# Turning the rotated keys of a tile by a transposing DMA instead of TensorE

## What is computed

```python
q = jnp.einsum('bsd,ed->bse', x, Wq).reshape(bsz, seqlen, HQ, D)
k = jnp.einsum('bsd,ed->bse', x, Wk).reshape(bsz, seqlen, HK, D)
v = jnp.einsum('bsd,ed->bse', x, Wv).reshape(bsz, seqlen, HK, D)
q = _rope(_rmsnorm(q, q_norm_w), pos)
k = _rope(_rmsnorm(k, k_norm_w), pos)
k_all = jnp.concatenate([k_cache[block_table], k], axis=1)
v_all = jnp.concatenate([v_cache[block_table], v], axis=1)
scores = jnp.einsum('bqhd,bkhd->bhqk', q, k_all) * SCALE
scores = jnp.where(valid, scores, -1e+30)
probs = jax.nn.softmax(scores, axis=-1)
o = jnp.einsum('bhqk,bkhd->bqhd', probs, v_all)
return jnp.einsum('bse,de->bsd', o, Wo)
```

## Time and profile before

| | us |
|---|---|
| median of three runs | 2203.47 |
| lowest and highest | 2203.23, 2203.65 |
| the profiled execution | 2202.7 |
| its span, first to last instruction | 2200.7 |
| TensorE busy | 2151.3 |
| VectorE busy | 1694.2 |
| ScalarE busy | 1486.1 |
| GpSimd busy | 1222.4 |
| mean granted TensorE clock | 0.995 |

### The profile page before, as it was taken

How to read it: one execution, slowest core, us unless ns; L and a number is a source line. 1 busy time by engine, 2 the same in 40 slices (tenths; PEclk the granted TensorE clock), 3 DMA queues, 4 the chain that set the end, 5 groups by cost and what they waited for, 6 DMA issues and landing times.

```text
span 2200.7 us, 61088 instructions
## 1 busy us (share of the span) xinstructions
PE 2151.3 (98%) x17966; PEld 1409.9 (64%) x17966; DVE 1694.2 (77%) x3917; ACT 1486.1 (68%) x4982; POOL 1222.4 (56%) x2070
## 2 busy tenths in 40 slices
PE   6989899999999999999999999999999999999998
PEld 3545466666666666666666666666666666666665
DVE  8785587777777777777777777787777777777785
ACT  5844487776676776777666666666777666666664
POOL 6002156655655556665566565666665565666563
PEclk9999999999999999999999999999999999999999
DMA  8988576766767666666778676666666666666563
GB/s 233 290 281 262 180 209 199 208 189 211 210 194 210 195 201 204 192 207 191 210 235 252 187 239 190 178 187 176 181 178 175 180 188 175 177 187 178 175 183 102
DMA packets 478831, 440.12 MB, mean 200 GB/s; under 512 B 52885, under 2 KB 407524, under 8 KB 477734
## 3 DMA queue, kind: packets, MB, share of 16 engines
q1 hardware_dynamic: 433062, 295.67, 46.0%
q0 software_dynamic: 40960, 134.25, 19.9%
q10 hardware_dynamic: 4480, 6.29, 1.0%
HBM read 377.21 MB, written 56.70 MB: 197 GB/s over the span
## 4 chain that ended last, share of the span: by engine, by line
PE 86%; DVE 1%; issue 0%; ACT 0%; DVEq 0%; ACTq 0%
PE PR L1323 22%; PE Op L1304 15%; PE WOp L1362 15%; PE Sp L1270 15%; PE PTp L1281 11%; PE TRp L1336 3%; PE Sp L1273 2%; PE Op L1286 1%; PE Op L1306 1%; PE TRp L1347 1%; DVE masked L1514 0%; PE WOp L1347 0%; ACT masked L1419 0%; DVE WoT L1573 0%; DVE OT L1532 0%
## 5 line engine op out<-in xcount | busy, mean ns | idle before, releaser
L735 POOL DMA_INDIRECT pages<-values_split,rows x512 | 525.0, 1025 | 104.0 <-issue 77.7
L1413 ACT ACTIVATE pts<-PTp 128x512 f16<-128x512 f32 x512 | 305.7, 597 | 364.4 <-PE PTp L1281 363.6
L1323 PE MATMUL PR<-Wt,xT 128*128 128x512 f16 x2232 | 539.0, 380 | 0.0
L1304 PEld LDWEIGHTS Op<-pts,pages 128*128 128x128 f16 x6144 | 385.3, 98 | 121.6 <-DVE OT L1532 4.4
L1304 PE MATMUL Op<-pts,pages 128*128 128x128 f16 x6144 | 426.7, 219 | 2.6 <-DVE OT L1532 2.4
L1270 PE MATMUL Sp<-pages,qT 128*128 128x512 f16 x1536 | 415.8, 380 | 6.5 <-PEq L185 6.5
L1514 DVE CUSTOM_DVE_ANT_0 masked<-Sp,mask 128x544 f32<-128x544 f32 x512 | 370.2, 723 | 60.2 <-PE Sp L1273 54.3
L1519 DVE TENSOR_TENSOR pts<-PTp,pts 128x512 f16<-128x512 f32 x512 | 351.6, 687 | 74.7 <-ACT pts L1413 74.1
L1419 ACT ACTIVATE masked<-masked,small 128x544 f32<-128x544 f32 x512 | 379.0, 740 | 8.1 <-DVE small L1514 7.7
L1362 PE MATMUL WOp<-WoT,OT 128*128 128x512 f16 x1536 | 377.5, 379 | 0.0
L1532 DVE TENSOR_TENSOR OT<-Op,OT 128x128 f16<-128x128 f32 x512 | 148.3, 290 | 265.5 <-ACT p L1407 261.9
(11 more groups left out here) (252 smaller groups left out, 3019.2 us busy)
## 6 DMA issues: line engine op xcount, KB each, us to landing
pages<-keys_transposed SPq DMA_DIRECT2D x2048, 64.0 KB
mask<-mask_rows SPq DMA_DIRECT2D x128, 128.0 KB, 3.8
v<-new_values SPq DMA_DIRECT2D x96, 128.0 KB
weights_split<-wdst SPq DMA_DIRECT2D x40, 256.0 KB, 4.7
keys_transposed<-pages SPq DMA_DIRECT2D x32, 256.0 KB, 4.7
values_split<-pages SPq DMA_DIRECT2D x16, 512.0 KB, 3.6
rope_s<-rope_table SPq DMA_DIRECT2D x32, 256.0 KB, 3.3
pages<-values_split,rows POOLq DMA_INDIRECT x512
```

The source lines that it names most:

```text
L735: nc.gpsimd.indirect_dma_start(out=vS[:, n % 2, c, :, :].rearrange("p l n -> p (l n)"), out_offset=None, in_=v_d, in_offset=bass.IndirectO ...
L1304: nc.tensor.matmul(o, vS[:, par, c, low, h * D:(h + 1) * D], pts[:, u % 2, part, c * P:(c + 1) * P], start=(k == 0), stop=False)
L1323: m = nc.tensor.matmul(bank(k), xT[:, c, xl, :], Wp[:, c, wl, GROUP_COL[k]:GROUP_COL[k] + HID], start=(i == 0), stop=(i == NPASS - 1))
L1413: nc.scalar.activation(pts[:, u % 2, 0, :], PTp[:, :], ACT.Copy).then_inc(G.pt_hi, 1)
```

## The change

The rotated keys (group 0) no longer go through TensorE. In slot 6 ScalarE copies `qr` to f16 in its natural order into a new buffer `split` and VectorE puts the low part beside it. At the end of slot 14 ScalarE's queue issues one transposing DMA from `split`, 128 partitions x 1024 f16, into `kTn`: eight blocks of 128x128, four heads high and four heads low. The next tile's first scores wait for it, and so does the next tile's write to `split`. The query groups are turned as before; their semaphore counts leave the keys out. To make room for `split`, four small tables of the first block move into the buffer of the output weights, which is free then.

```diff
+QUERY_GROUPS = len(NORMED) - 1
...
-    turn={5: 0, 6: 1, 10: 3, 12: 4, 14: 5}, turned={6: 0, 7: 1, 11: 3, 13: 4, 15: 5},
+    keys=14, turn={6: 1, 10: 3, 12: 4, 14: 5}, turned={6: 0, 7: 1, 11: 3, 13: 4, 15: 5},
...
+        split = sb("split", [P, 2, HID], F16)
...
-        seqf = sb("seqf", [P, B], F32)
-        wq_b = sb("wq_b", [P, D], F32)
-        wk_b = sb("wk_b", [P, D], F32)
...
-        stacked = sb("stacked", [P, 3 * P // 2], F32)
...
-        jump = scr[:, 2880:2944]
+        seqf, wq_b, wk_b, stacked = scr[:, 2880:2944], scr[:, 7168:7296], scr[:, 8064:8192], scr[:, 3392:3584]
...
+            def turn_no(ti, k):
+                return ti * QUERY_GROUPS + NORMED.index(k) - 1
...
                         if u % UPT == 0 and u > 0:
-                            pe.wait_ge(G.tr_lo, len(NORMED) * (u // UPT))
+                            pe.wait_ge(G.tr_lo, QUERY_GROUPS * (u // UPT))
+                            pe.wait_ge(G.keys_turned, 16 * (u // UPT))
...
-                        if m_ >= 1:
-                            pe.wait_ge(G.tr_lo, m_)
+                        if turn_no(ti, k) >= 1:
+                            pe.wait_ge(G.tr_lo, turn_no(ti, k))
...
                     def rotated_high(ti, tt, k):
-                        a.wait_ge(G.tr_done, norm_no(ti, k) + 1)
+                        if k == 0:
+                            a.wait_ge(G.rope_done, norm_no(ti, k) + 1)
+                            if ti >= 1:
+                                a.wait_ge(G.keys_turned, 16 * ti)
+                            nc.scalar.activation(split[:, 0, :], qr[:, norm_no(ti, k) % 2, :], ACT.Copy).then_inc(G.split_high, 1)
+                            return
+                        a.wait_ge(G.tr_done, turn_no(ti, k) + 1)
...
+                            if sl == plan["keys"]:
+                                a.wait_ge(G.split_low, ti + 1)
+                                a.dma_start(kTn[:, 1 - tt, :, :].rearrange("p l (h n) -> p (l h) n", h=KVH), split[:, :, :].rearrange("p l n -> p (l n)"), transpose=True).then_inc(G.keys_turned, 16)
...
-                        if m_ >= 2:
-                            v.wait_ge(G.tr_done, m_ - 1)
+                        before, kb = divmod(m_ - 2, len(NORMED))
+                        if m_ >= 2 and kb == 0:
+                            v.wait_ge(G.split_low, before + 1)
+                        if m_ >= 2 and kb >= 1:
+                            v.wait_ge(G.tr_done, turn_no(before, NORMED[kb]) + 1)
...
                     def rotated_low(ti, tt, k):
-                        v.wait_ge(G.tr_hi, norm_no(ti, k) + 1)
+                        if k == 0:
+                            v.wait_ge(G.split_high, ti + 1)
+                            V.tensor_tensor(split[:, 1, :], qr[:, norm_no(ti, k) % 2, :], split[:, 0, :], ALU.subtract).then_inc(G.split_low, 1)
+                            return
+                        v.wait_ge(G.tr_hi, turn_no(ti, k) + 1)
```

More of the change, by code:

```diff
@@ L167, in build @@
             "proj_done", "sq_done", "var_done", "rstd_done", "scaled", "rope_part", "rope_done",
-            "tr_done", "tr_hi", "tr_lo", "vn_hi", "vn_lo", "y_done", "yin_loaded", "y_stored", "xT_loaded")}
+            "tr_done", "tr_hi", "tr_lo", "split_high", "split_low", "keys_turned", "vn_hi", "vn_lo", "y_done", "yin_loaded", "y_stored", "xT_loaded")}
         G = type("G", (), block_sems)
@@ L298, in _ @@
                                  (ifreq, inv_freq.rearrange("(o n) -> o n", o=1).to_broadcast([P, D // 2])),
-                                 (wq_b[:, :], q_norm_w.rearrange("(o n) -> o n", o=1).to_broadcast([P, D])),
-                                 (wk_b[:, :], k_norm_w.rearrange("(o n) -> o n", o=1).to_broadcast([P, D]))):
+                                 (wq_b, q_norm_w.rearrange("(o n) -> o n", o=1).to_broadcast([P, D])),
+                                 (wk_b, k_norm_w.rearrange("(o n) -> o n", o=1).to_broadcast([P, D]))):
                     sp.dma_start(dst, src).then_inc(G.tables_loaded, 16)
@@ L1163, in rotated @@
                     nt = 1 - tt
-                    if k == 0:
-                        return TRp[:, :].rearrange("p (h n) -> p h n", h=4), kTn[:, nt, part, :].rearrange("p (h n) -> p h n", h=4)
                     h = NORMED.index(k) - 1
```

## The result

| | before | changed |
|---|---|---|
| median, us | 2203.56 | 2227.06 |
| lowest to highest (6 runs each) | 2203.18 to 2206.09 | 2223.66 to 2238.62 |
| profiled execution | 2202.7 | 2227.7 |
| its span | 2200.7 | 2225.7 |

The changed kernel takes 1.0115 times as long, interval 1.0102 to 1.0128: 23.5 us more, where 13.6 us less was forecast. The time lies inside the stated range, but on the other side of the kernel before.

The account below looks back on a forecast made before the run. TensorE, busy for all 59.78 us of a tile period, was taken as the bound. 2203.5 - 13.6 (transposes) + 0 (GpSimd's margin) + 0 (transposing DMA) = 2189.9, said as 2190 us; range 2188 to 2265.

Parts of the forecast that it names:

- What is removed: Slot 5: TensorE's four transposes of the rotated keys go, 0.44 us in each of 31 tiles, 13.6 us less.
- Edits with one answer: Slot 6: key copy and subtraction, now with SBUF sources, cost within some 0.1 us what they did; moved tables cost nothing.
- VectorE's low probabilities, 0.56 us in hand: After slot 6: they end at 1384.19, the next turning of probabilities comes at 1384.75, so TensorE does not wait.
- GpSimd's margin of 0.17 us: End of slot 6: GpSimd's addition ends 0.17 us before TensorE's earlier query turn; holds narrowly, at most 3 us in all.
- The issue, free up to 2.66 us: ScalarE's queue, slot 14: DMA issue is hidden up to 2.66 us from the exponentials' end; beyond, each microsecond costs 31.
- The landing: Next tile's first scores: keys land in 3 to 4.7 us, window 4.27 to 5.10 us, so stall 0.
- Rival C: First scores of each tile: keys land late, TensorE stalls; 2261 us at a 7.0 us landing, 2435 at 12.2; chance 0.35.
- Rival D: Slot 6: GpSimd's addition or VectorE holds it for the whole 0.44 us, no gain, 2200 to 2204 us; chance 0.03.
- The tables: First block: tables moved into the weight buffer are the same instructions at another address, cost nothing.

Follow-up runs that it names:

- the slot 10 kernel: The changed kernel with the transposing DMA at the end of slot 10 instead of 14, subtraction left in place: 2210.87 us against 2204.4, ratio 1.0026.

## Why the prediction was wrong

**What is removed: right.** The 0.44 us step is gone from 31 tiles; where nothing else is late, the period is 59.34 us as worked out.

**Edits with one answer: the step that failed.** It said that the subtraction with SBUF sources costs within 0.1 us of the old 686 ns, "VectorE's is 682 ns for 512 f32 columns", and that VectorE "is off the path there". The row of 682 ns is a VectorE instruction with two SBUF sources, but all 155 of them stand ahead of the GpSimd addition of their own group, which waits for them, and none overlaps an addition. The subtraction stands beside the addition of the next group: the earlier trace rows show that addition at 1382.14 to 1383.41 in the very slot. It took 1650 ns. The old subtraction, 0.17 us behind the same addition, read one operand from PSUM and took 0.69 us; the change is in where its operand lies, which the step took for free. The Trainium skill, *SBUF — State Buffer*, section Who interferes with whom, has a rule against just this: a VectorE instruction with two SBUF inputs contends with a GpSimd instruction that reads SBUF, and the order of issue decides which of them is blocked. The trace agrees: the addition came first and is as long as ever, 1.27 us, and the subtraction takes 1650 ns against 681; the prediction did not weigh this rule.

**VectorE's low probabilities, 0.56 us in hand: wrong by the same 0.97 us.** 1650 - 686 = 0.96 us is more than 0.56, and the remainder is 0.40 us. The margin itself was read 0.14 us too wide: it ran from VectorE's end to TensorE's start, and the chain shows 0.14 us between the two. Had the subtraction been entered with its length, this line of the prediction would have given 2203.5 - 13.6 + 31 x 0.40 = 2202.3, and with these 0.14 us 2206.6. That is 3.1 us above before; the slot 10 kernel, in which only this remains, lies 5.7 us above it (1.0026 of 2204.4). The difference is about what its first and fifteenth periods take beyond the others, 1.3 and 0.8 us.

**GpSimd's margin of 0.17 us: held.** No wait of the query turn for GpSimd is listed in any tile.

**The issue, free up to 2.66 us: held.** It is 1.25 us in the median. Two of the 31 are longer than the bound, 3.08 and 2.82 us, and ScalarE's next instruction then waits 2.15 and 2.03 us instead of 0.81. No wait of the output products follows, since the issue starts 0.9 us before the point that the bound counts from. It starts with the exponentials, not behind them, and in the other tiles ScalarE's next instruction is as late as it was, 0.81 us of waiting for TensorE as in the earlier trace rows. Issue, exponentials and the output's high part in a good tile of the changed kernel:

```profile
1255.43 1.25 ACTq L1499 DMA_TRANSPOSE kTn<-split  x1
1255.50 0.74 ACT L1419 ACTIVATE masked<-masked,small 128x544 f32<-128x544 f32 x1
...
1257.14 0.28 ACT L1428 ACTIVATE OT<-Op 128x128 f16<-128x128 f32 x1 [0.81 <-PE Op L1286]
```

**The landing: right in the middle, wrong at the end of the range.** The trace gives it for the changed kernel, minimum, median and maximum in us:

```profile
DMA to landing us min/median/max: 3.5/4.3/11.4
```

The median of 4.3 us lies inside the 3 to 4.7 that were taken, and 21 of 31 tiles don't wait. The other ten do. This is the second step that failed: "the stall 0, with little to spare" took one number for 31 transfers; the window of 4.27 to 5.10 us (5.17 in a late tile of the changed kernel) had to hold each of them, beside whatever else the DMA engines have at that moment. The earlier trace rows had shown that they are not all alike, share 0.00 in one tile and 1.01 in another. The worst tile is the one where SyncE's queue fetches 2 MB of weights at the same time:

```profile
1187.57 1.28 SPq L789 DMA_DIRECT2D Wt<-weights_split  x2
1187.76 1.35 ACTq L1499 DMA_TRANSPOSE kTn<-split  x1
...
1199.28 1.44 PE L1270 MATMUL Sp<-pages,qT 128*128 128x512 f16 x3 [6.20 <-DMA kTn<-split]
```

**Rival C.** Its direction came true, and a part of its mechanism, the keys that land late. Its picture did not: it had all 31 tiles alike at 2.3 us, 71 us in all, and the runs show 9 to 15 tiles with 12 to 19 us in all. Nor did eight blocks take the 10.5 us that the prediction worked out for them in a row: they landed in 4.3 us in the median. The other half of the loss, S, was in no rival. Rival D spoke of VectorE and GpSimd holding slot 6, but for the whole 0.44 us at most and with margins that "speak against it", chance 0.03. In the slot 10 kernel VectorE did hold it, for 0.56 us.

**The tables: nothing, as said.**

In sum, of the changed kernel's loop of 30 periods: transposes gone - 13.2, S + 16.8, L and what goes with it + 16.6, together + 20.2 us; the 4.6 us ahead of the loop are within what unchanged kernels differ by. A later subtraction alone left L, an earlier DMA alone left S (and in slot 12 made others late); slot 10 or 8 together with the later subtraction left neither. Not settled is why slot 12 in particular makes value products wait, and which transfers a turning one holds up.

## What to carry to other kernels

When an instruction's operand moves from PSUM to SBUF, its price is not that of the nearest row of the same shape but that of a row with the same neighbours: look at what GpSimd does in that microsecond. Set a margin ahead of a transfer against the longest landing of 31, not the median, and read the DMA engines' load in the window of every tile. Where two causes stand behind one loss, undo both at once as well as singly: here each single cure looked like a failure, and together, with the DMA in slot 10, they gave 12.7 us.

## What was not expected of the hardware

**A VectorE instruction beside GpSimd** takes 1650 ns instead of 681, in 31 of 31 cases with a spread of 9 ns, if both its operands lie in SBUF; GpSimd's addition does not become longer (1262 to 1277 ns, before 1262 to 1281).

**A turning DMA loads the engines more than a plain one.** It takes 256 KB in 1056 packets instead of 144 and 1.25 us of issue instead of 0.47; in the third microsecond after the issue the share was 1.43 instead of 0.91; and in one tile with late products the core's traffic 4 to 6 us after the issue was 98 GB/s at a share over 1. Which transfers it slows is not listed. The Trainium skill, *Advanced Engine Details and Errata*, section X-Bar Transpose (TRN2), says that such DMAs are as fast as others; the median landing, 4.3 us, is no slower than plain rows of 2.4 to 4.7, but the same transfer plain in the same place brought the kernel from 1.0093 to 0.9965.

**A wait costs more than its length.** In the longest stall TensorE's granted clock fell from 1.00, its level of 2.4 GHz, to 0.50, that of 1.2 GHz, while it stood idle, and was back at full only some 3 us after the work had begun again at 1199.28 (windows of 1 us, columns as in the earlier trace rows):

```profile
1193.00:1194.00 1.00, 0.08 (x2) 0.00 (x0) 0.11 (x1) 0.45 (x2) 0.55 (x3) 1.00 1.15 365
1196.00:1197.00 1.00, 0.00 (x0) 0.00 (x0) 0.00 (x0) 0.00 (x0) 0.00 (x0) 0.50 1.18 251
1201.00:1202.00 1.00, 1.00 (x6) 0.66 (x5) 1.00 (x3) 0.23 (x1) 0.00 (x0) 0.50 1.11 309
1202.00:1203.00 1.00, 1.00 (x6) 0.43 (x5) 0.77 (x2) 1.00 (x3) 0.00 (x0) 0.87 1.11 295
```

The scores behind it took 1.44 us instead of 0.81, and the period with that stall was 67.7 us, 7.9 longer than the late one before, for a wait of 6.2; 0.1 of the 7.9 is the collision's.
